# One of two column chunks of the expert rows arrives already turned, as two f16 halves, by a transposing DMA

## The chip, the core and the metric

One of the eight cores of one Trainium2 chip runs the whole program. The metric is the device time of one execution in microseconds (us). The engines are PE (TensorE, matrix products; its weight loads are listed as PEld), DVE (VectorE), ACT (ScalarE), POOL (GpSimd), and SP (SyncE), which here only issues DMAs and waits. An engine's name with a q (SPq, POOLq) is its instruction queue.

## The reference

```
x = x + L0_xattn(ctx, layernorm(x))          # 16 heads
x = x + L0_ffn(layernorm(x))                 # all 8 experts, weighted by their counts
x = x + L1_xattn(layernorm(x), ctx, ctx, mask)
x = x + L1_ffn(layernorm(x), ...)

def L1_ffn(x, W1, b1, W2, b2, Wg, bg):       # 3584 tokens, 256 columns, 8 experts, hidden 512
    gate_logits = xt @ Wg.T + bg
    w, idx = top_k(gate_logits, 2);  w = softmax(w)
    h = relu(einsum('td,ehd->eth', xt, W1) + b1[:, None, :])
    y = einsum('eth,eoh->eto', h, W2) + b2[:, None, :]
    comb = (one_hot(idx, 8) * w[..., None]).sum(axis=1)
    return einsum('eto,te->to', y, comb)
```

The kernel works out only the two experts that a token chose. The change lies in this last part: the rows that are sent to the experts, and how an expert reads them.

## The kernel before, in words

**Three phases.** The attention phase (up to some 450 us), the middle phase (dense mixture, second attention, layer norm and routing; some 450 to 776 us), and the expert stage (some 776 to 985 us). Inside a phase each engine runs its own written-out list of instructions; semaphores order them.

**Middle phase, one step per batch of 112 tokens, 32 batches.** The steps are pipelined: in step u the mixture works on batch u, attention on batches u-4 and u-5, the norm and the gate on u-6 (`ur`), and the sending on u-7 (`uk`). After the last mixture seven more steps drain this pipeline. For a routed batch ACT writes the normalised row `rows[.., 0:256]` in fp32 (L1689), TensorE turns it (L1604), ACT and DVE split the turned row into f16 halves for the gate (`xT_hi` L1698, `xT_lo` L1830). POOL writes the token number (L1518), the combine weights (L1524) and the slots (L1526), updates the running counts (`cum`, L1528), and one step later sends the row twice by indirect DMA (`scatter`, L1475) to the `dispatch` array in DRAM: a row is 272 fp32 words (256 values, 8 weights, the token number, padding). After the last batch a count of tokens on PE (L1640) and a chain of small DVE operations (L1845 to L1902) make the table that tells the expert stage where its rows lie.

**Expert stage.** The sent rows are cut into 63 units of 128 rows. Units 0 to 47 go in pairs of the same expert (24 turns, `paired`); 15 single units make the last 8 turns. For each turn SP loads the rows (L2000 a pair, L2004 a single unit) into one of 4 slots of `rows_e`; a slot is free when the turn four before has written its `y` (`y_rdy`, the wait at L1998, whose instruction is listed as L61). In turns 4 to 18 SP also copies the W1 halves of one single unit inside SBUF (L2009, two copies of 256 KB). PE turns the rows (`turn_rows`, L2048: for a pair two chunks of 128 columns times two units, four fp32 transposes) in the middle of the `up` of the turn before; ACT and DVE split the turned values into f16 halves (`x_hi` L2143, `x_lo` L2187); `up` makes 24 products a pair turn (L2065, hi*hi, hi*lo, lo*hi), ACT applies bias and relu, and `down` (L2100) makes 24 more. DVE adds the bias and scales by the weight (L2209, L2214), and POOL adds each unit's `y` into the output by an indirect DMA (L2035). Such an add may have to wait until the adds of the units before have landed (L2027 to L2033), where the expert changes.

Of the kernel before, what the change touches and what calls it, by code (L numbers as in the profile page):

```python
# [19 lines left out]
E = 8  # L20
# [69 lines left out]
def attention_phase(nc, ctx, dram, keep):  # L90
# [153 lines left out]
    with nc.Block(no_gpsimd_drain=True) as block:  # L244
# [179 lines left out]
        def _(pe):  # L424
# [219 lines left out]

            def maxima_turned(b):            run_steps(pe, step)
# [610 lines left out]
def middle_phase(nc, ctx, dram, keep):  # L1256
# [53 lines left out]
    def reuse(*shape):  # L1310
# [17 lines left out]
    x3 = we[:].rearrange("p c e h -> p (c e h)")[0:S, DC * D * E // 2:DC * D * E // 2 + 2 * D].rearrange("p (n d) -> p n d", d=D)  # L1328
# [5 lines left out]
    w_hi, w_lo = keep["w_hi"], keep["w_lo"]  # L1334
    route_w = sb("route_w", [128, DC, E], F32)
# [18 lines left out]
        cum_rdy token_rdy scattered0 scattered1 scattered2 scattered3 x3_out0 x3_out1 pads_out w_in0 w_in1 w_hi_rdy w_lo_rdy rows_set late_in tally_done table  # L1354
# [41 lines left out]
    with nc.Block(no_gpsimd_drain=True) as block:  # L1396
# [60 lines left out]
        def _(pool):  # L1457
# [27 lines left out]
            def step(t, u, on):  # L1485
# [8 lines left out]
                if r:  # L1494

                    ur = u - LAG_ROUTE
                    v = cnt(t, ur, 1, 1)
                    rstd("ag3", "eps3", "rs3", 1, v)
                    wait(pool, m["rs3"], v)
                    wait(pool, m["x3n_rdy"], cnt(t, ur - 1, 1, 1))  # L1500
# [12 lines left out]
                if r:  # L1513

                    ur = u - LAG_ROUTE
                    wait(pool, scattered[ur % ROW_SLOTS], sent(t, ur - ROW_SLOTS))
                    apart(pool)
                    nc.gpsimd.tensor_scalar(rows[:, ur % ROW_SLOTS, AT_TOKEN:AT_TOKEN + 1], rows[:, ur % ROW_SLOTS, AT_TOKEN:AT_TOKEN + 1],  # L1518
                                            float(ROW_SLOTS * S), None, ALU.add).then_inc(m["token_rdy"], 1)
# [16 lines left out]
        def _(pe):  # L1536
# [24 lines left out]
            def step(t, u, on):  # L1561
# [38 lines left out]
                if r:  # L1600
                    wait(pe, m["x3n_rdy"], cnt(t, ur, 1, 1))
# [47 lines left out]
        def _(act):  # L1649
# [7 lines left out]
            def step(t, u, on):  # L1657
# [25 lines left out]
                if r:  # L1683
# [5 lines left out]
                    nc.scalar.activation(rows[:, ur % ROW_SLOTS, 0:D], x3[:, ur % 2, :], ACT.Identity, bias=ln_shift[:, 1, :],  # L1689
# [5 lines left out]
                if r:  # L1695
                    b0 = (t * TURN + ur) * S
                    wait(act, m["x3nT_done"], cnt(t, ur, 1, 1))
                    nc.scalar.activation(xT_hi[:, :, bass.ds(b0, S)], psum[:, 7, 0:DC * S].rearrange("p (c s) -> p c s", c=DC), ACT.Copy).then_inc(m["x3hi_rdy"], 1)  # L1698

# [3 lines left out]
        def _(dve):  # L1703
# [32 lines left out]
            def step(t, u, on):  # L1736
# [80 lines left out]
                if o:  # L1817
# [3 lines left out]
                    wait(dve, m["x3n_rdy"], cnt(t, uo - 2, 1, 1))  # L1821
# [84 lines left out]
def expert_phase(nc, ctx, dram, keep):  # L1906
# [20 lines left out]
    rows = sb("rows_e", [128, ROW_TURNS, PAIR, ROW], F32)  # L1927
    token_at = sb("token_at", [128, TOKEN_TURNS, PAIR], U32)
    x_hi = sb("x_hi", [128, 2, DC, PAIR * UNIT], F16)
    x_lo = sb("x_lo", [128, 2, DC, PAIR * UNIT], F16)  # L1930
# [13 lines left out]
    names = """pads_sent pads_rdy own_in passed rows_in0 rows_in1 rows_in2 rows_in3 xT_done xhi_rdy xlo_rdy up_done0 up_done1 h_rdy0 h_rdy1  # L1944
# [3 lines left out]
    rows_in = [m[f"rows_in{n}"] for n in range(ROW_TURNS)]  # L1948
# [37 lines left out]
    with nc.Block(no_gpsimd_drain=True) as block:  # L1986

        @block.sync
        def _(sp):
            sp.sem_inc(m["pads_rdy"], 1)  # L1990
            for n in range(TURNS):
# [4 lines left out]
                else:  # L1996
                    sp.wait_ge(m["pads_rdy"], 2)
                wait(sp, m["y_rdy"], finished(n - ROW_TURNS + 1))  # L1998
                if paired(n):
                    sp.dma_start(rows[:, n % ROW_TURNS, :, :],  # L2000
                                 dram["dispatch"][bass.ds(start[0], PAIR * UNIT), :].rearrange("(s p) r -> p s r", p=UNIT)).then_inc(rows_in[n % ROW_TURNS], 16)
                else:
                    for s in units(n):
                        sp.dma_start(rows[:, n % ROW_TURNS, s, :], dram["dispatch"][bass.ds(start[s], UNIT), :]).then_inc(rows_in[n % ROW_TURNS], 16)  # L2004
# [36 lines left out]
        def _(pe):  # L2041
            def turn_rows(n):
# [3 lines left out]
                for kc in range(DC):  # L2046
                    for s in units(n):
                        last = nc.tensor.transpose(psum[:, 0, (kc * PAIR + s) * UNIT:(kc * PAIR + s + 1) * UNIT],  # L2048
                                                   rows[:, n % ROW_TURNS, s, kc * 128:(kc + 1) * 128], ident[:, :])
                last.then_inc(m["xT_done"], 1)  # L2050

            def up_pair(n, e, then):

                wait(pe, m["xlo_rdy"], n + 1)
                for c in range(HC):
# [7 lines left out]
                    for w, x in ((w1_hi, x_hi), (w1_hi, x_lo), (w1_lo, x_hi)):  # L2063
                        for kc in range(DC):
                            last = nc.tensor.matmul(psum[:, 1 + c // 2, c % 2 * PAIR * UNIT:(c % 2 + 1) * PAIR * UNIT],  # L2065
                                                    w[:, bass.ds(e, 1), kc, c * 128:(c + 1) * 128].rearrange("p o h -> p (o h)"),
                                                    x[:, n % 2, kc, :], start=(done == 0), stop=(done == 3 * DC - 1))
# [4 lines left out]
            def up_unit(n, s, then):  # L2072
# [4 lines left out]
                if s == 0:  # L2077
                    wait(pe, m["xlo_rdy"], n + 1)
                for c in range(HC):
# [5 lines left out]
                    for w, x in ((own_hi, x_hi), (own_hi, x_lo), (own_lo, x_hi)):  # L2085
                        for kc in range(DC):
                            last = nc.tensor.matmul(up_bank(s, c), w[k][:, kc, c * 128:(c + 1) * 128], x[:, n % 2, kc, s * UNIT:(s + 1) * UNIT],
# [49 lines left out]
        def _(act):  # L2137
            def high_x(n):
# [4 lines left out]
                nc.scalar.activation(x_hi[:, n % 2, :, 0:width], psum[:, 0, 0:DC * PAIR * UNIT].rearrange("p (c s) -> p c s", c=DC)[:, :, 0:width],  # L2143
                                     ACT.Copy).then_inc(m["xhi_rdy"], 1)
# [38 lines left out]
        def _(dve):  # L2183
            def low_x(n):
                width = len(units(n)) * UNIT
                wait(dve, m["xhi_rdy"], n + 1)
                nc.vector.tensor_tensor(x_lo[:, n % 2, :, 0:width], psum[:, 0, 0:DC * PAIR * UNIT].rearrange("p (c s) -> p c s", c=DC)[:, :, 0:width],  # L2187
                                        x_hi[:, n % 2, :, 0:width], ALU.subtract).then_inc(m["xlo_rdy"], 1)
# [16 lines left out]
            def finish(n, s, e):  # L2205
# [8 lines left out]
                nc.vector.tensor_scalar(y[:, unit % SLOTS, :], y_sum[:, s, :], rows[:, n % ROW_TURNS, s, bass.ds(e + AT_W, 1)], None,  # L2214
                                        ALU.mult).then_inc(m["y_rdy"], 1)

            def tokens(n):
# [3 lines left out]
                                      rows[:, n % ROW_TURNS, 0:len(units(n)), AT_TOKEN:AT_TOKEN + 1]).then_inc(m["token_rdy"], 1)  # L2221
# [147 lines left out]
```

## Time and profile before

| | us |
|---|---|
| median of 3 runs (lowest, highest) | 984.41 (982.87, 990.5) |
| the profiled execution, its own time | 987.03 |
| its span, first to last instruction | 984.9 |
| PE busy / PEld busy | 900.4 / 668.7 |
| DVE / ACT / POOL busy | 730.3 / 543.4 / 551.4 |
| mean granted TensorE clock, of full speed | 0.958 |

The span is what the trace shows; the execution took 2.1 us more than its span. Busy times are shares of the whole program, which has phases with different limits, so they say little by themselves: the phase in question has to be looked at alone.

### The profile page before, as it was taken

The page shows a single profiled execution, that of the slowest core. Times are in us where ns is not written, and L with a number is a line of the kernel's source. Part 1 is how long each engine was busy: PE and PEld are TensorE (multiplying, and loading weights), DVE is VectorE, ACT ScalarE, POOL GpSimd, SP SyncE. Part 2 cuts the span into 40 slices and gives each one's busy share as a digit, 9 for nine tenths or more (in the row PEclk, how much of TensorE's full clock was granted, in tenths as well). Part 3 has the DMA queues.
Part 4 walks back from the last instruction along what each step waited for, and adds up shares of the span by engine and source line. Part 5 has one row for each costly group of instructions (what it writes and reads, how often), then busy time and mean ns, then how long its engine had stood idle before and what let it go on. Part 6 is the DMA issues. An engine that isn't in the chain of part 4 may idle for free. (4 is left out here: it accounts for less than half of the span.)

```text
span 984.9 us, 31478 instructions
## 1 busy us (share of the span) xinstructions
PE 900.4 (91%) x10664; PEld 668.7 (68%) x10664; DVE 730.3 (74%) x2071; ACT 543.4 (55%) x1068; POOL 551.4 (56%) x897
## 2 busy tenths in 40 slices
PE   4799999999999999986999999999976399999993
PEld 2477777777777777754466666666644289889892
DVE  6688888888888888866778888888865356666773
ACT  3377777777777777654044444444443065555551
POOL 6655555565555555401037777777776535556536
PEclk9899999999999999987999999999996599999997
DMA  5644554445444454331565555665552348786535
GB/s 157 178 128 142 144 147 134 135 144 147 125 139 141 142 142 144 94 105 47 141 179 174 183 186 186 189 191 184 175 190 90 120 100 197 176 187 105 96 64 59
DMA packets 107278, 140.56 MB, mean 143 GB/s; under 512 B 23929, under 2 KB 92592, under 8 KB 106928
## 3 DMA queue, kind: packets, MB, share of 16 engines
q1 hardware_dynamic: 94594, 121.38, 41.3%
q0 software_dynamic: 12528, 17.18, 9.7%
q8 instruction: 89, 1.46, 0.6%
q14 instruction: 67, 0.55, 0.2%
HBM read 93.38 MB, written 38.35 MB: 134 GB/s over the span
## 5 line engine op out<-in xcount | busy, mean ns | idle before, releaser
L999 DVE TENSOR_REDUCE smax<-psum 112x2 f32<-112x750 f32 x240 | 216.3, 933 | 24.5 <-PE psum L439 24.4
L840 ACT ACTIVATE probsT<-psum 125x896 f32<-125x896 f32 x173 | 158.7, 917 | 22.0 <-PE psum L454 20.6
L2035 POOL DMA_INDIRECT out_dram<-y,token_at x63 | 101.6, 1612 | 93.9 <-DMA out_dram<-y,token_at 42.2
L1733 DVE SCALAR_TENSOR_TENSOR acc<-psum,neg_bias,acc 128x448 f32<-128x448 f32 x112 | 75.9, 680 | 10.9 <-PE psum L1556 9.3
L1475 POOL DMA_INDIRECT dispatch_dram<-rows,slots_at x64 | 64.0, 1000 | 28.4 <-issue 28.4
L439 PE MATMUL psum<-k_stack,q_stack 63*128 63x375 f16 x480 | 69.3, 326 | 3.9 <-DVE smax L999 2.8
L1556 PE MATMUL psum<-xT_hi,we_hi 128*128 128x448 f16 x256 | 70.2, 356 | 1.1 <-ACT we_hi L1655 1.1
L476 PE MATMUL psum<-probsT,v_aug 125*32 125x112 f32 x2688 | 70.2, 260 | 0.1
L1556 PE MATMUL psum<-xT_lo,we_hi 128*128 128x448 f16 x256 | 69.8, 355 | 0.0
L1556 PE MATMUL psum<-xT_hi,we_lo 128*128 128x448 f16 x256 | 69.7, 354 | 0.0
L476 PEld LDWEIGHTS psum<-probsT,v_aug 125*32 125x32 f32 x2688 | 63.5, 110 | 8.9 <-ACT v_aug L866 8.5
L454 PE MATMUL psum<-q_stack,k_stack 64*128 64x112 f16 x1384 | 63.8, 211 | 2.9 <-DMA q_stack<-neg_max 2.9
L2167 ACT ACTIVATE h<-psum,b 128x256 f32<-128x256 f32 x96 | 40.1, 471 | 38.9 <-PE psum L2065 34.3
L573 PE MATMUL psum<-wv_hi,we 128*125 128x256 f16 x384 | 59.3, 276 | 0.9 <-ACT we L860 0.8
L357 POOL TENSOR_SCALAR ln_var<-ln_mv 112x1 f32<-112x1 f32 x32 | 7.2, 224 | 92.8 <-DVE ln_mv L1011 92.8
L408 POOL TENSOR_TENSOR k_lo<-we,k_hi 128x375 f16<-128x375 f32 x64 | 55.9, 874 | 5.1
L454 PEld LDWEIGHTS psum<-q_stack,k_stack 64*128 64x128 f16 x1384 | 44.3, 95 | 21.1 <-issue 12.6
L1662 ACT ACTIVATE probs<-probs,exp_bias 112x375 f32<-112x375 f32 x32 | 19.4, 607 | 67.8 <-DVE exp_bias L1756 67.8
L553 PE MATMUL psum<-we,wk_hi 128*128 128x375 f16 x256 | 53.8, 334 | 2.9 <-ACT we L860 1.5
L2203 DVE TENSOR_TENSOR h_lo<-h,h_hi 128x512 f16<-128x512 f32 x63 | 41.3, 688 | 17.0 <-ACT h_hi L2153 13.5
L1591 PE MATMUL psum<-ctx_rows,probsT 125*112 125x256 f32 x192 | 50.3, 401 | 2.9 <-issue 2.9
L365 POOL TENSOR_TENSOR we<-we 128x750 f16<-128x750 f32 x32 | 51.5, 1609 | 1.1 <-ACT we L847 1.1
(298 smaller groups left out, 2448.3 us busy)
## 6 DMA issues: line engine op xcount, KB each, us to landing
k_stack<-k_hi_dram SPq DMA_DIRECT2D x64, 188.0 KB, 2.8
we<-in_ctxT_dram SPq DMA_DIRECT2D x32, 375.0 KB, 3.5
ctxT<-in_ctxT_dram SPq DMA_DIRECT2D x32, 375.0 KB
ctx_rows<-in_ctx_dram SPq DMA_DIRECT2D x32, 375.0 KB
w_raw<-in_w_dram SPq DMA_DIRECT2D x32, 256.0 KB, 3.9
rows_e<-dispatch_dram SPq DMA_DIRECT2D x24, 272.0 KB
k_hi_dram<-k_hi SPq DMA_DIRECT2D x32, 188.0 KB, 2.8
k_lo_dram<-k_lo SPq DMA_DIRECT2D x32, 188.0 KB, 2.7
```

What stands on the lines that cost most here:

```text
L408: nc.gpsimd.tensor_tensor(k_lo[:, u % 2, mc, 0:KV], k_full[:, mc, :], k_hi[:, u % 2, mc, 0:KV], ALU.subtract).then_inc(m["klo_ready"], 1)
L439: last = nc.tensor.matmul(psum[:, pair_bank(s) + a, 0:KV], queries(rows, b4, s, 128), keys_at(rows, b4, s, 0, KV), start=True, stop=True)
L454: last = nc.tensor.matmul(psum[:, a, r * S:(r + 1) * S], keys_at(rows, b4, 4 * hg + r, c * KC, 128), queries(rows, b4, 4 * hg + r, S), sta ...
L476: last = nc.tensor.matmul(bank_d[32 * j:32 * j + 32, g * S:(g + 1) * S], v_aug[:, b4d, cc, h, :], probsT[:, b2d, cc, h // 8, h % 2, h // 2 ...
L553: last = nc.tensor.matmul(bank_a[:, 0:KV], w[:, kc, mc * 128:(mc + 1) * 128], x[:, b2a, kc, :], start=(n == 0), stop=(n == 3 * DC - 1))
L573: last = nc.tensor.matmul(bank[0:KC, n * D:(n + 1) * D], x[:, b2a, kc, cc * KC:(cc + 1) * KC], w[:, kc, :], start=(done == 0), stop=(done ...
L840: nc.scalar.activation(probsT[:, p, c, hg, :, :, :].rearrange("p k h q -> p k (h q)"), psum[0:KC, 0:2, 0:4 * S], ACT.Exp, scale=float(HD) ...
L999: nc.vector.reduce_max(smax[:, (u - LAG_B) % 2, 2 * (s % 4) + s // 4::PAIRS], psum[0:S, pair_bank(s):pair_bank(s) + 2, 0:KV], AX.X).then_i ...
L1475: nc.gpsimd.indirect_dma_start(dram["dispatch"], bass.IndirectOffsetOnAxis(slots_at[:, b % ROW_SLOTS, n:n + 1], 0), rows[:, b % ROW_SLOTS, ...
L1556: last = nc.tensor.matmul(psum[:, mix_bank(t, u, k), 0:GT], w[:, kc, e, hc * 128:(hc + 1) * 128], x[:, kc, bass.ds(g0, GT)], start=(n == 0 ...
L1733: nc.vector.scalar_tensor_tensor(out, psum[:, mix_bank(t, u, k), 0:GT], neg_bias[:, hc, e:e + 1], out, ALU.max, ALU.add).then_inc(m["acc_r ...
L2035: nc.gpsimd.indirect_dma_start(dram["out"], bass.IndirectOffsetOnAxis(token_at[:, unit // PAIR % TOKEN_TURNS, unit % PAIR:unit % PAIR + 1] ...
```

## The change

In the middle phase the first 128 columns of a sent row are no longer fp32: their 512 bytes hold 128 f16 high halves and 128 f16 low halves. ACT writes the second 128 columns as before, the first 128 into a small buffer `x3n`, and the high half as a copy of it; POOL makes the low half by a subtraction. In the expert stage SP loads columns 128 and on as before (144 words of a row in place of 272), and issues two transposing DMAs for a pair turn (four for a turn of two single units), which bring the two halves of the first chunk into `x_hi[0]` and `x_lo[0]` with the columns on the partitions. TensorE turns only the second chunk, and ACT and DVE split only that. `x_hi[0]` and `x_lo[0]` have 4 slots in place of 2. PE waits for the transposed halves (`x_in`) at the start of `up`. From turn 4 on SP issues a turn's transposing DMAs ahead of its wait for `y`, in turns 0 to 3 behind the rows. The first hunk takes out a second, never called definition of a function.

```diff
@@ middle phase, POOL
+                if k:
+                    uk = u - LAG_SEND
+                    wait(pool, m["x3hi_rdy"], cnt(t, uk, 2, 2))
+                    nc.gpsimd.tensor_tensor(rows_lo[:, uk % ROW_SLOTS, :], x3n[:, uk % 2, :], rows_hi[:, uk % ROW_SLOTS, :],
+                                            ALU.subtract).then_inc(m["row_rdy"], 1)
@@ middle phase, PE
                     for kc in range(DC):
-                        last = nc.tensor.transpose(psum[:, 7, kc * S:(kc + 1) * S], rows[:, ur % ROW_SLOTS, kc * 128:(kc + 1) * 128], ident[0:S, 0:S])
+                        half_row = x3n[:, ur % 2, :] if kc == 0 else rows[:, ur % ROW_SLOTS, 128:D]
+                        last = nc.tensor.transpose(psum[:, 7, kc * S:(kc + 1) * S], half_row, ident[0:S, 0:S])
@@ middle phase, ACT
-                    nc.scalar.activation(rows[:, ur % ROW_SLOTS, 0:D], x3[:, ur % 2, :], ACT.Identity, bias=ln_shift[:, 1, :],
+                    nc.scalar.activation(rows[:, ur % ROW_SLOTS, 128:D], x3[:, ur % 2, 128:D], ACT.Identity, bias=ln_shift[:, 1, :],
+                                         scale=ln_rstd[:, 1, :]).then_inc(m["x3n_rdy"], 1)
+                    wait(act, m["row_rdy"], cnt(t, ur - 2, 2, 2))
+                    nc.scalar.activation(x3n[:, ur % 2, :], x3[:, ur % 2, 0:128], ACT.Identity, bias=ln_shift[:, 1, :],
                                          scale=ln_rstd[:, 1, :]).then_inc(m["x3n_rdy"], 1)
...
+                    nc.scalar.activation(rows_hi[:, ur % ROW_SLOTS, :], x3n[:, ur % 2, :], ACT.Copy).then_inc(m["x3hi_rdy"], 1)
@@ expert stage, SP
+                def transposed():
+                    wait(sp, up_done[0], 2 * (n - ROW_TURNS + 1))
+                    wait(sp, up_done[1], 2 * (n - ROW_TURNS + 1 - DOUBLES))
+                    for s, at in enumerate(start):
+                        width = PAIR * UNIT if paired(n) else UNIT
+                        for half, x in enumerate((x_hi, x_lo)):
+                            sp.dma_start(x_of(x, n, 0, s * UNIT, width), halves[bass.ds(at, width), half * 128:(half + 1) * 128],
+                                         transpose=True).then_inc(x_in[n % ROW_TURNS], 16)
+
+                if n >= ROW_TURNS:
+                    transposed()
                 wait(sp, m["y_rdy"], finished(n - ROW_TURNS + 1))
                 if paired(n):
                     sp.dma_start(rows[:, n % ROW_TURNS, :, :],
-                                 dram["dispatch"][bass.ds(start[0], PAIR * UNIT), :].rearrange("(s p) r -> p s r", p=UNIT)).then_inc(rows_in[n % ROW_TURNS], 16)
+                                 dram["dispatch"][bass.ds(start[0], PAIR * UNIT), 128:ROW].rearrange("(s p) r -> p s r", p=UNIT)).then_inc(rows_in[n % ROW_TURNS], 16)
...
+                if n < ROW_TURNS:
+                    transposed()
@@ expert stage, PE, turn_rows and up_pair
-                for kc in range(DC):
-                    for s in units(n):
-                        last = nc.tensor.transpose(psum[:, 0, (kc * PAIR + s) * UNIT:(kc * PAIR + s + 1) * UNIT],
-                                                   rows[:, n % ROW_TURNS, s, kc * 128:(kc + 1) * 128], ident[:, :])
+                for s in units(n):
+                    last = nc.tensor.transpose(psum[:, 0, s * UNIT:(s + 1) * UNIT], rows[:, n % ROW_TURNS, s, 0:128], ident[:, :])
...
+                wait(pe, x_in[n % ROW_TURNS], 2 * rows_arrived(n))
                 wait(pe, m["xlo_rdy"], n + 1)
```

SP's list for one of the turns 4 to 18 before (TENSOR_LOAD is a look-up in the table):

```order
L1964 TENSOR_LOAD table
L1964 ISA x2
L2000 ISA
L2000 DMA rows_e<-dispatch_dram 128x2x272
L2009 ISA
L2009 DMA xT_lo<-w_hi 128x1024
L2009 REGISTER_ALU
L2009 DMA spare_w<-w_lo 128x1024
```

and with the change:

```order
L1977 TENSOR_LOAD table
L1977 ISA x2
L2021 ISA
L2021 DMA_TRANSPOSE x_hi<-dispatch_dram 128x256
L2021 DMA_TRANSPOSE x_lo<-dispatch_dram 128x256
L2028 ISA
L2028 DMA rows_e<-dispatch_dram 128x2x144
L2039 ISA
L2039 DMA xT_lo<-w_hi 128x1024
L2039 REGISTER_ALU
L2039 DMA spare_w<-w_lo 128x1024
```

Two more DMAs stand in SP's list for a turn, between the look-ups and the load of the rows.

PE's list in the middle of the `up` of a pair turn before:

```order
L2065 MATMUL psum<-x_hi,w_lo 128x256
L2048 MATMUL psum<-ident,rows_e 128x128 x4
L2065 ISA
L2065 MATMUL psum<-x_hi,w_hi 128x256
L2065 MATMUL psum<-x_lo,w_hi 128x256 x2
```

and with the change:

```order
L2094 MATMUL psum<-x_hi,w_lo 128x256
L2077 MATMUL psum<-ident,rows_e 128x128 x2
L2094 ISA
L2094 MATMUL psum<-x_hi,w_hi 128x256
L2094 MATMUL psum<-x_lo,w_hi 128x256 x2
```

Two of the four transposes are gone; nothing else on PE has moved.

POOL's list in a step of the middle phase before, from the sending of the batch before on:

```order
L1475 DMA dispatch_dram<-rows,slots_at 30208x272 x2
L1511 TENSOR_TENSOR w_lo<-w_raw,w_hi 128x512
L1518 TENSOR_SCALAR rows<-rows 112x1
L1524 TENSOR_SCALAR rows<-unscaled,first_w 112x8
L1526 CAST slots_at<-slots 112x2
L1528 TENSOR_TENSOR cum<-cum,chosen 112x8
```

and with the change:

```order
L1475 DMA dispatch_dram<-rows,slots_at 30208x272 x2
L1508 TENSOR_TENSOR rows<-we,rows 112x128
L1516 TENSOR_TENSOR w_lo<-w_raw,w_hi 128x512
L1523 TENSOR_SCALAR rows<-rows 112x1
L1529 TENSOR_SCALAR rows<-unscaled,first_w 112x8
L1531 CAST slots_at<-slots 112x2
L1533 TENSOR_TENSOR cum<-cum,chosen 112x8
```

One subtraction has come in ahead of the weight split and the counts.

## Rows read from the trace of the kernel before

**Rows 1.** Stretches of the program: busy us per engine, granted clock, DMA share, GB/s.

```profile
core 0: us, PE busy (x) PEld busy (x) DVE busy (x) ACT busy (x) POOL busy (x), PEclk, DMA share, GB/s
500.00:720.00 220.00, 219.40 (x1317) 144.76 (x1315) 180.30 (x765) 95.12 (x233) 154.30 (x328) 1.00 0.59 182
720.00:777.80 57.80, 30.86 (x146) 20.97 (x146) 31.72 (x192) 18.54 (x46) 38.75 (x82) 0.70 0.36 114
800.00:888.00 88.00, 87.60 (x800) 78.53 (x799) 55.37 (x122) 51.52 (x109) 49.04 (x30) 1.00 0.81 187
888.00:928.00 40.00, 39.76 (x388) 35.97 (x386) 25.86 (x62) 22.99 (x49) 23.22 (x15) 1.00 0.58 98
```

**Rows 2.** Chain that ended last, its first and last pieces: start, us, what.

```profile
928.60 0.33 DVE y_sum L2209
...
932.11 3.87 DMA out_dram<-y,token_at
...
976.83 3.56 DMA out_dram<-y,token_at
```

**Rows 3.** Timeline of PE, pair turns: start, us, line, operation, count.

```profile
785.95 1.06 PE L2048 MATMUL psum<-ident,rows_e 128*128 128x128 f32 x4
786.80 0.53 PE L2065 MATMUL psum<-x_hi,w_hi 128*128 128x256 f16 x2
...
906.13 0.60 PE L2048 MATMUL psum<-ident,rows_e 128*128 128x128 f32 x4
906.57 0.38 PE L2065 MATMUL psum<-x_hi,w_hi 128*128 128x256 f16 x2
...
911.81 0.60 PE L2048 MATMUL psum<-ident,rows_e 128*128 128x128 f32 x4
```

**Rows 4.** Timeline of SP's queue, turns with own copies.

```profile
804.56 0.39 SPq L2000 DMA_DIRECT2D rows_e<-dispatch_dram  x1
...
810.26 0.38 SPq L2000 DMA_DIRECT2D rows_e<-dispatch_dram  x1
811.35 0.50 SPq L2009 DMA_DIRECT2D xT_hi<-w_hi  x1
811.97 0.53 SPq L2009 DMA_DIRECT2D we<-w_lo  x1
```

**Rows 5.** Waits of SP's queue, 800 to 885 us: total us, times, longest.

```profile
SPq L61 <- DVE y L2214: 16.8, 11, 2.5
```

**Rows 6.** Issues of the pads to the output by SP: ns min/median/max.

```profile
L1417 SPq DMA_DIRECT2D out_dram<-in_pads_dram x5: 589/597/597, 478.1 to 480.7; - x5
```

**Rows 7.** DMA queue of SP (q1), 800 to 888 us: packets, MB, share of 16 engines.

```profile
q1 hardware_dynamic: 8663, 12.31, 43.8%
```

**Rows 8.** The same, 888 to 928 us.

```profile
q1 hardware_dynamic: 1952, 1.95, 18.3%
```

**Rows 9.** The expert stage's start: SP's first load, PE's first transposes and products.

```profile
777.80 21.58 SPq L2000 DMA_DIRECT2D rows_e<-dispatch_dram  x5
...
780.77 1.12 PE L2048 MATMUL psum<-ident,rows_e 128*128 128x128 f32 x4 [5.53 <-DMA rows_e<-dispatch_dram]
783.39 0.60 PE L2065 MATMUL psum<-x_hi,w_hi 128*128 128x256 f16 x2 [1.50 <-issue]
```

**Rows 10.** Timeline of POOL, middle phase: a steady step, the draining, the last batches.

```profile
721.45 0.22 POOL L1481 TENSOR_SCALAR ln_var<-ln_mv 112x1 f32<-112x1 f32 x1 [0.66 <-DVE ln_mv L1745]
...
729.50 0.22 POOL L1481 TENSOR_SCALAR ln_var<-ln_mv 112x1 f32<-112x1 f32 x1 [0.19 <-DVE ln_mv L1745]
...
769.15 0.19 POOL L1528 TENSOR_TENSOR cum<-cum,chosen 112x8 f16<-112x8 f16 x1
```

**Rows 11.** Two subtractions of POOL: ns min/median/max.

```profile
L408 POOL TENSOR_TENSOR k_lo<-we,k_hi x64: 847/886/902, 17.0 to 412.1; 128x375 f16<-128x375 f32 x64
L1511 POOL TENSOR_TENSOR w_lo<-w_raw,w_hi x32: 1149/1170/1177, 486.9 to 751.0; 128x512 f16<-128x512 f32 x32
```

**Rows 12.** Groups by shape, ACT: busy us, mean ns, idle before.

```profile
L1689 ACT ACTIVATE rows<-we,ln_shift,ln_rstd 112x256 f32<-112x256 f32 x32 | 19.2, 600 | 18.8 <-POOL ln_shift L1502 18.8
```

More of the change, by code:

```diff
@@ L1334, in middle_phase @@
     w_hi, w_lo = keep["w_hi"], keep["w_lo"]
+    rows_hi, rows_lo = (rows[:].bitcast(F16)[:, :, n * 128:(n + 1) * 128] for n in range(2))
     route_w = sb("route_w", [128, DC, E], F32)
@@ L1499, in step @@
                     wait(pool, m["rs3"], v)
-                    wait(pool, m["x3n_rdy"], cnt(t, ur - 1, 1, 1))
+                    wait(pool, m["x3n_rdy"], cnt(t, ur - 1, 2, 2))
                     apart(pool)
@@ L1698, in step @@
                     nc.scalar.activation(xT_hi[:, :, bass.ds(b0, S)], psum[:, 7, 0:DC * S].rearrange("p (c s) -> p c s", c=DC), ACT.Copy).then_inc(m["x3hi_rdy"], 1)
+                    wait(act, m["x3n_rdy"], cnt(t, ur, 2, 2))
+                    apart(act)
+                    nc.scalar.activation(rows_hi[:, ur % ROW_SLOTS, :], x3n[:, ur % 2, :], ACT.Copy).then_inc(m["x3hi_rdy"], 1)
             steps(act, step)
@@ L1925, in expert_phase @@
     b1, b2, pad_at, pad_rows, table = (keep[k] for k in ("b1", "b2", "pad_at", "pad_rows", "table"))
-    rows = sb("rows_e", [128, ROW_TURNS, PAIR, ROW], F32)
+    rows = sb("rows_e", [128, ROW_TURNS, PAIR, ROW - 128], F32)
     token_at = sb("token_at", [128, TOKEN_TURNS, PAIR], U32)
-    x_hi = sb("x_hi", [128, 2, DC, PAIR * UNIT], F16)
-    x_lo = sb("x_lo", [128, 2, DC, PAIR * UNIT], F16)
+    x_hi = [sb(f"x_hi{kc}", [128, slots, PAIR * UNIT], F16) for kc, slots in enumerate((ROW_TURNS, 2))]
+    x_lo = [sb(f"x_lo{kc}", [128, slots, PAIR * UNIT], F16) for kc, slots in enumerate((ROW_TURNS, 2))]
+    halves = dram["dispatch"].bitcast(F16)
     h = sb("h", [128, PAIR, HC, UNIT], F32)
@@ L1947, in expert_phase @@
     m = {n: sem("x_" + n) for n in names}
-    rows_in = [m[f"rows_in{n}"] for n in range(ROW_TURNS)]
+    rows_in, x_in = ([m[f"{k}{n}"] for n in range(ROW_TURNS)] for k in ("rows_in", "x_in"))
     added = [m[f"added{n}"] for n in range(SLOTS)]
@@ L2066, in up_pair @@
                                                     w[:, bass.ds(e, 1), kc, c * 128:(c + 1) * 128].rearrange("p o h -> p (o h)"),
-                                                    x[:, n % 2, kc, :], start=(done == 0), stop=(done == 3 * DC - 1))
+                                                    x_of(x, n, kc, 0, PAIR * UNIT), start=(done == 0), stop=(done == 3 * DC - 1))
                             done += 1
@@ L2077, in up_unit @@
                 if s == 0:
+                    wait(pe, x_in[n % ROW_TURNS], 2 * rows_arrived(n))
                     wait(pe, m["xlo_rdy"], n + 1)
@@ L2142, in high_x @@
                 width = len(units(n)) * UNIT
-                nc.scalar.activation(x_hi[:, n % 2, :, 0:width], psum[:, 0, 0:DC * PAIR * UNIT].rearrange("p (c s) -> p c s", c=DC)[:, :, 0:width],
-                                     ACT.Copy).then_inc(m["xhi_rdy"], 1)
+                nc.scalar.activation(x_of(x_hi, n, 1, 0, width), psum[:, 0, 0:width], ACT.Copy).then_inc(m["xhi_rdy"], 1)
             def high_h(n, s):
@@ L2220, in tokens @@
                 nc.vector.tensor_copy(token_at[:, n % TOKEN_TURNS, 0:len(units(n))].rearrange("p (n o) -> p n o", o=1),
-                                      rows[:, n % ROW_TURNS, 0:len(units(n)), AT_TOKEN:AT_TOKEN + 1]).then_inc(m["token_rdy"], 1)
+                                      rows[:, n % ROW_TURNS, 0:len(units(n)), AT_TOKEN - 128:AT_TOKEN - 127]).then_inc(m["token_rdy"], 1)
             def experts(n):
```

29 lines of the change are left out of this document (15 added, 14 removed).

## The prediction

> **What bounds the kernel now.** I began with the chain of waits. It names only the end [rows 2]: from 928.60 us on the program follows the indirect adds into the output, nine landings in a row (first and last are shown), each add waiting for the one before. What starts this chain is the `y` of the last pair turn, so what comes earlier counts only as far as it moves that point. The stretches [rows 1] show what does: from 800 to 928 us PE is busy for 87.60 of 88 us and 39.76 of 40 us at the full granted clock, while DVE, ACT and POOL have a third or more to spare. The timeline [rows 3] has one pair turn from transpose to transpose, 906.13 to 911.81, so 5.68 us. DMA is the second thing to see there: its share is 0.81 while the weights of the single units are copied, 0.58 afterwards. The middle phase is PE's too (219.40 of 220 us), but from 720 to 777.8 us it drains: PE is busy for 30.86 of 57.80 us, and the chain passes from engine to engine.
>
> **TensorE.** The four transposes of a pair turn hold PE from 906.13 to 906.57 [rows 3], 0.44 us; two are left, so 0.22 us a turn, and a turn of 5.46 us if PE goes on setting it. Ahead of the point at 928.60 us lie the transposes of turns 1 to 24: 24 x 0.22 = 5.3 us is the most that PE can give. The later single turns save as much, but there the chain of adds is waited for, not PE, so that counts nothing. The narrower split on ACT and DVE lies beside PE and counts nothing.
>
> **The stage's start.** From the first transpose to the first product it takes 783.39 - 780.77 = 2.62 us [rows 9]; TensorE is still slow there, and the four transposes of the next turn take 786.80 - 785.95 = 0.85 us [rows 3], so half of them saves 0.43, and the narrower splits a little more: up to 0.9 us. But PE now needs the transposed halves as well, issued behind the rows. The first load was issued at 777.80 and used at 780.77, 2.97 us later [rows 9]. With the second half issued 1.2 to 2 us after it, it arrives at about 782 to 783, about when the split is done. I take -0.5; the ends are -0.9 and +3.
>
> **SP, where the change adds.** In a turn with copies of weights SP's turn is 810.26 - 804.56 = 5.70 us [rows 4]. Its free time is what it waits for `y`: 16.8 us in 11 waits, 1.53 us each [rows 5]; if the other four of the 15 turns truly have none, 1.12 a turn. So its own work is 4.17 us, or 4.58. Two transposing DMAs come on top, ahead of the wait, and the load of the rows is queued behind them: SP's turn becomes that work plus 2T, T being the time that SP takes to issue one. The trace has no such issue. The nearest rows are plain issues: 0.38 us for 256 rows, 0.50 and 0.53 for the copies [rows 4], 0.59 for DRAM to DRAM, the dearest undisturbed one [rows 6]. Below 0.38 nothing speaks for it; above, no row bounds it, so the upper end is a rival. A transposing DMA has more to lay out than a plain one, so I take 0.6. That makes 4.17 + 1.2 = 5.37 us, under PE's 5.46, or 4.58 + 1.2 = 5.78, over it. I take 5.6, between the two: 15 turns x (5.60 - 5.70) = -1.5 us. The other nine turns save 9 x 0.22 = 2.0 us.
>
> **The DMA engines.** From 888 to 928 us SP's queue takes 18.3% of 40 us for four pair loads and six single ones, seven pairs' worth [rows 8]: 1.05 us of all engines for 272 KB, 265 GB/s. In the earlier stretch, where the copies of weights raise the queue's share to 43.8% [rows 7], a turn leaves 0.19 x 5.70 = 1.08 us free, and the shorter rows give back between nothing (if a row costs the same) and 0.49 us (by bytes). The transposed 128 KB thus have room for 1.08 to 1.57 us, which is 121 to 84 GB/s; at the rate of the row loads they take 0.49. I cost this at nothing, with that cover. The page DMA: Bandwidth & Descriptors of the Trainium skill, section Latency and other measured facts, gives 261 GB/s for a transposing DMA with a non-contiguous middle dimension; by it the halves would take 0.50 us, an estimate, and no run here shows it yet.
>
> **The middle phase.** POOL's subtraction is 128 columns wide. Its like took 886 ns for 375 columns and 1170 ns for 512 [rows 11], 2.07 ns a column, so 0.37 us. In a steady step POOL waits 0.66 us for DVE [rows 10] and PE sets the pace: nothing, with that cover. While the pipeline drains the wait is 0.19 us, so 0.18 comes through in each of four steps, and in the last two, where POOL's own list leads to the counts that end at 769.15, all of it: 4 x 0.18 + 2 x 0.37 = 1.5 us; the ends are 0.7 and 3. ACT's one normalisation of 256 columns (600 ns) [rows 12] becomes two of 128. If each cost half the sum is unchanged, if each cost as much as the whole, 0.6 us more in some seven draining steps: 0 to 4.2 us. The columns are the same in sum, so I take 0.5, near the first. The copy to f16 stands behind `xT_hi`, where ACT next waits for DVE: nothing.
>
> **The sum.** -1.5 - 2.0 - 0.5 + 1.5 + 0.5 = -2.0 us. The profiled execution took 987.03 us (span 984.9), which is 2.6 above the median of 984.41 and inside its range; against it the change would make 985.0, against the median 982.4. I forecast **982 us**. With T at 0.38 (PE's 5.46 us holds in 15 turns, so -3.6 in place of -1.5) and the cheap ends of the middle phase it is 979; with SP's turn at 5.78 and the dear ends 994.
>
> **Rival 1, the slower side: SP's queue sets the turn.** Place: the two transposing DMAs ahead of the load of the rows, turns 4 to 18. Price: 15 x (4.17 + 2T - 5.70). T = 1.5 gives 15 x 1.47 = 22 us, and with the other terms (-2.0 - 0.5 + 2.0) 1006 us; T = 2 gives +37 and 1021. It decides from T = 0.65 on, and 9.8 us (1%) are reached at T = 1.11. For it: SP has only these 1.1 to 1.5 us a turn to give, and the load of the rows stands behind both transposing DMAs. Against it: no plain issue is over 0.6 us undisturbed. Chance 0.38, of which 0.26 beyond T = 1.11.
>
> **Rival 2: the turning is slow in the DMA engines.** A pair turn has four halves of 128 x 128. If they are turned one after another, PE gets one turn's worth every four of these times, and from 1.37 us each (5.46 / 4) that sets the turn. By rows, if the two DMAs of a turn follow one another, each like the first load's 2.97 us, a turn is 5.94: 24 x (5.94 - 5.70) = 5.8, and with -0.5 and +2.0 it makes 992; if each of the four took that long, 11.9 us a turn and over 1100. If they are spread but move at a quarter of the row loads' rate, 1.98 us a turn, it overruns the room by 0.4 to 0.9 us: +6 to +13 in 15 turns, 990 to 997. For it: each half is 256 rows of only 256 bytes. Against it: DMA is idle for 0.19 to 0.42 of the time. Chance 0.14, of which 0.12 slower by over 1%. The page VectorE: DVE Perf Modes of the Trainium skill, section The three transpose paths, speaks against the change: 390 ns for such a block on TensorE, 1309 ns by the DMA crossbar; four of these would be an estimated 5.24 us, just within PE's turn. The trace's 0.11 us a transpose in a stream [rows 3] is cheaper still than the page's figure for TensorE.
>
> **Rival 3: faster by over 1%.** The nine landings sum to 36.7 us; if lighter loads brought all to the shortest, 3.56 us [rows 2], that gave another 4.6; with SP hidden (15 x 0.24 = 3.6, and 2.0 and 0.5) and a free middle phase it reaches 10.7 us and 974. All of it must come together. Chance 0.06. That TensorE would still turn both chunks is excluded by its list of instructions.
>
> **How the numbers follow.** The forecast has 0.42, its own range 977 to 990. A measurement of this kernel can tell about 1%, 9.8 us, from no change. Slower: 0.26 + 0.12 = 0.38. Faster: 0.06. The same: 0.42 + 0.12 + 0.02 = 0.56. The range reaches from 975 (leaving out most of rival 3) to 1015 (T up to about 1.8).
>
> **What would show it.** The step on PE is right if the transposes of a pair turn hold it for 0.22 us and turns are 5.46 to 5.7 us apart. T is read off SP's queue; its waits for `y` from 800 to 885 us should fall from 16.8 us to near nothing. Rival 1 shows as no such wait left, turns over 5.8 us, and PE waiting for `rows_e`; rival 2 as PE waiting for `x_hi` and a DMA share near 1; the middle phase as a longer stretch from 720 us to the table. I am wrong if T is over 1.1 us, or if a transposing DMA holds up the others in its queue.

## The result, and the profile after

The changed kernel takes 1017.18 us (median of 4 runs, 1013.88 to 1017.99), the kernel before in the same comparison 985.67 us (4 runs, 982.87 to 990.5): a ratio of 1.030, 95% interval 1.027 to 1.033. It is slower by 31.5 us, and outside the predicted range of 975 to 1015. The profiled execution after took 1013.88 us with a span of 1012.1; before it was 987.03 and 984.9, so 27 us is what the two traces can explain.

The stretches, in the columns of [rows 1]:

```profile
core 0: us, PE busy (x) PEld busy (x) DVE busy (x) ACT busy (x) POOL busy (x), PEclk, DMA share, GB/s
500.00:720.00 220.00, 218.39 (x1311) 144.03 (x1310) 180.29 (x764) 106.90 (x284) 163.93 (x353) 1.00 0.59 181
720.00:778.86 58.86, 30.07 (x146) 20.12 (x146) 31.37 (x190) 20.77 (x58) 41.07 (x88) 0.72 0.35 111
800.00:888.00 88.00, 73.08 (x633) 61.86 (x630) 42.70 (x103) 39.94 (x91) 38.95 (x25) 0.98 0.75 154
888.00:928.00 40.00, 36.63 (x316) 31.90 (x317) 20.33 (x50) 18.79 (x44) 19.41 (x13) 0.96 0.71 123
```

Up to 720 us PE is nearly as full as before (218.39 us for 219.40); ACT and POOL are busy 11.8 and 9.6 us longer there, with the added work. The draining stretch is 1.06 us longer (58.86 for 57.80). Then PE, which had been full from 800 to 888 us, is idle for 14.9 of 88 us, and no other engine took over: DVE, ACT and POOL all do less, the DMA share fell from 0.81 to 0.75, and the granted clock is nearly the same (0.98 for 1.00). An idle stretch with no busy engine in it points to a queue. PE's waits name one (total us, times, longest): first those of before for 800 to 928 us, then those after the change for 800 to 928 and for 928 to 1012:

```profile
PE psum L2048 <- DMA rows_e<-dispatch_dram: 0.2, 1, 0.2
```

```profile
PE psum L2077 <- DMA rows_e<-dispatch_dram: 17.7, 13, 2.6
```

```profile
PE psum L2077 <- DMA rows_e<-dispatch_dram: 11.4, 6, 2.6
```

PE waits for the rows, which are loaded by a plain DMA, and not for the transposed halves. The rows are late because their load stands behind two transposing DMAs in SP's queue. SP's timeline of one turn with copies of weights, in answer to [rows 4]:

```profile
861.18 1.12 SPq L2021 DMA_TRANSPOSE x_hi<-dispatch_dram  x1
862.44 1.21 SPq L2021 DMA_TRANSPOSE x_lo<-dispatch_dram  x1
863.85 0.42 SPq L2028 DMA_DIRECT2D rows_e<-dispatch_dram  x1
865.00 0.51 SPq L2039 DMA_DIRECT2D xT_lo<-w_hi  x1
865.63 0.53 SPq L2039 DMA_DIRECT2D spare_w<-w_lo  x1
868.01 1.16 SPq L2021 DMA_TRANSPOSE x_hi<-dispatch_dram  x1
```

From 861.18 to 863.85 the two transposing DMAs hold SP for 2.67 us, T = 1.33 us each with the register work between them; the whole turn is 868.01 - 861.18 = 6.83 us. The rest, 4.16 us, is SP's other work, as it was read from before. All issues of the kind together (ns min/median/max), and under them what SP waits for `y` in all of 800 to 1012 us, where [rows 5] had 16.8 us in 85 us:

```profile
L2021 SPq DMA_TRANSPOSE x_hi<-dispatch_dram x39: 767/1125/2579, 779.4 to 985.9; - x39
L2021 SPq DMA_TRANSPOSE x_lo<-dispatch_dram x39: 695/1147/2290, 780.8 to 987.0; - x39
```

```profile
SPq L2028 <- DVE y L2242: 1.3, 1, 1.3
```

SP has next to no free time left. In the turns of single units it is worse, since each has four transposing DMAs, and these take as long for 128 rows as the others for 256:

```profile
938.28 1.12 SPq L2021 DMA_TRANSPOSE x_hi<-dispatch_dram  x1
939.53 1.14 SPq L2021 DMA_TRANSPOSE x_lo<-dispatch_dram  x1
940.80 1.15 SPq L2021 DMA_TRANSPOSE x_hi<-dispatch_dram  x1
942.08 1.15 SPq L2021 DMA_TRANSPOSE x_lo<-dispatch_dram  x1
943.43 0.95 SPq L2032 DMA_DIRECT2D rows_e<-dispatch_dram  x2
945.72 1.11 SPq L2021 DMA_TRANSPOSE x_hi<-dispatch_dram  x1
```

That is 7.44 us a turn where PE had taken some 6.0 before (from turn 25 to 31). Where SP is not the bound, PE's gain is there as predicted. In turns 20 to 23, which have no copies, the transposes of two turns in a row, in answer to [rows 3], stand 5.46 us apart, and the first product follows 0.22 us after them:

```profile
909.88 0.38 PE L2077 MATMUL psum<-ident,rows_e 128*128 128x128 f32 x2
910.10 0.38 PE L2094 MATMUL psum<-x_hi,w_hi 128*128 128x256 f16 x2
...
915.34 0.38 PE L2077 MATMUL psum<-ident,rows_e 128*128 128x128 f32 x2
```

The table puts the loss in its place: the start of the transposes of some turns, read from PE's timeline of each kernel; e1 to e9 are the experiments told below. Turns 4 to 18 have the copies, 24 to 31 the single units.

| kernel | turn 0 | turn 4 | turn 19 | turn 24 | turn 31 | span | us a turn, 4 to 19 | us a turn, 24 to 31 |
|---|---|---|---|---|---|---|---|---|
| before | 780.77 | 803.09 | 889.10 | 917.49 | 960.36 | 984.9 | 5.73 | 6.12 |
| after | 781.29 | 803.76 | 909.88 | 939.61 | 995.15 | 1012.1 | 7.07 | 7.93 |
| e1 | 781.11 | 803.82 | 889.81 | 920.68 | 974.54 | 991.5 | 5.73 | 7.69 |
| e2 | 781.76 | 804.06 | 905.04 | 934.00 | 981.81 | 1000.0 | 6.73 | 6.83 |
| e3 | 781.87 | 806.57 | 894.27 | 922.66 | 965.64 | 987.8 | 5.85 | 6.14 |
| e4 | 780.31 | 803.41 | 891.62 | 918.91 | 960.53 | 983.9 | 5.88 | 5.95 |
| e5 | 782.73 | 806.44 | 890.37 | 917.66 | 958.60 | 987.2 | 5.60 | 5.85 |
| e7 | 781.81 | 804.37 | 910.39 | 938.09 | 979.83 | 1003.2 | 7.07 | 5.96 |
| e9 | 782.84 | 805.83 | 891.06 | 918.36 | 959.45 | 982.6 | 5.68 | 5.87 |

After against before: +0.7 us up to turn 4, +20.1 from 4 to 19, +1.3 to turn 24 (the gain of 0.22 us in each of four turns, and then the first single turn, late by 2.2), +12.7 from 24 to 31. At the end 7.6 us come back: the adds, which before came last by a long chain [rows 2], are now caught up by the products, and the chain of waits begins only here:

```profile
1002.07 0.50 DVE y L2242
...
1007.73 1.55 POOL out_dram L2065
```

### The profile page after: what moved, and what is told of

The parts are those of the page before. It is cut to its first block and busy times, and to the rows that moved or that the text cites. A ratio compares the mean times of both kernels' runs of the same rounds, so it can differ in the third digit from the quotient of the medians.

```text
span 1012.1 us, 31638 instructions
## 1 busy us (share of the span) xinstructions
PE 904.3 (89%) x10601; PEld 663.8 (66%) x10601; DVE 721.5 (71%) x2071; ACT 551.3 (54%) x1132; POOL 560.3 (55%) x929
## 5 line engine op out<-in xcount | busy, mean ns | idle before, releaser
L2065 POOL DMA_INDIRECT out_dram<-y,token_at x63 | 98.9, 1571 | 122.6 <-DVE y L2242 73.0
L1475 POOL DMA_INDIRECT dispatch_dram<-rows,slots_at x64 | 64.0, 1000 | 28.6 <-issue 28.6
L2216 DVE TENSOR_TENSOR x_lo<-psum,x_hi 128x256 f16<-128x256 f32 (+1 forms) x32 | 13.4, 420 | 57.1 <-ACT x_hi L2173 42.6
```

Of the source, the lines that this page charges most:

```text
L2065: nc.gpsimd.indirect_dma_start(dram["out"], bass.IndirectOffsetOnAxis(token_at[:, unit // PAIR % TOKEN_TURNS, unit % PAIR:unit % PAIR + 1] ...
```

## The experiments

Theory A: SP issues a transposing DMA for some 1.13 us (1.3 with its register work) whatever its size, and this serial time sets the turn, in turns 4 to 18 and in the single turns. Theory B: the turning is slow in the DMA engines, and SP is only held up by it. Theory C: the middle phase carries a good part. Each ratio is to the kernel before on the same chip in the same comparison.

**e2, time on SP and nothing else.** To the kernel before, look-ups of a table entry are added at the head of SP's turns:

```diff
             for n in range(TURNS):
+                if n >= ROW_TURNS:
+                    for _ in range(4 * len(loads(n))):
+                        look_up(sp, 1, PAIR * n, 0, DISPATCH_ROWS)
```

> The kernel before with nothing but time added on SP: four more look-ups of the table (some 0.7 us each) at the head of each pair turn from turn 4 on, eight in each turn of single units; no DMA is added or moved, and nothing else differs. Theory A: SP's list is 4.2 + 2.7 = 6.9 us, so turns 4 to 18 are 6.7 to 7.2 us apart and the time is that of the changed kernel, 1008 to 1022 us, with PE waiting for rows_e. Theory B: SP's time alone does little: under 995 us.

Measured: 1001.99 us, ratio 1.015 (1.011 to 1.018). A turn from 4 to 19 took 6.73 us, and PE waited for the rows as in the changed kernel. SP's turn, and PE's waits from 800 to 928 us:

```profile
848.80 0.39 SPq L2003 DMA_DIRECT2D rows_e<-dispatch_dram  x1
849.90 0.50 SPq L2012 DMA_DIRECT2D xT_lo<-w_hi  x1
850.52 0.54 SPq L2012 DMA_DIRECT2D spare_w<-w_lo  x1
855.20 0.39 SPq L2003 DMA_DIRECT2D rows_e<-dispatch_dram  x1
```

```profile
PE psum L2051 <- DMA rows_e<-dispatch_dram: 11.0, 11, 2.0
```

The turn shown is 855.20 - 848.80 = 6.40 us; the loads of turns 4 to 18 are 6.81 us apart on average, 2.6 us above SP's work of 4.16 or 4.17. So 2.6 us of pure SP time in a pair turn, without a byte more on the DMA engines, gives 15.9 of the 20.8 us by which turn 19 came late after the change. The time expected was too high: it came out 6 us under the range. In the single turns the look-ups cost less than the four transposing DMAs (6.83 us a turn for 7.93), and the changed kernel's longer issues (up to 2.58 us) have no counterpart here.

**e1, the copies on another queue.** The changed kernel, with the look-up and the two copies of a single unit's weights issued by ACT:

```diff
-                if ROW_TURNS <= n < ROW_TURNS + SINGLES:
-                    k = n - ROW_TURNS
-                    e = look_up(sp, 0, PAIR * DOUBLES + k, 0, E - 1)
-                    for own, w in ((own_hi, w1_hi), (own_lo, w1_lo)):
-                        sp.dma_start(own[k], w[:, bass.ds(e, 1), :, :].rearrange("p o c h -> p (o c) h")).then_inc(m["own_in"], 16)
...
+                    if c == 1 and ROW_TURNS <= n < ROW_TURNS + SINGLES:
+                        k = n - ROW_TURNS
+                        own_e = look_up(act, 0, PAIR * DOUBLES + k, 0, E - 1)
+                        act.dma_start(own_hi[k], w1_hi[:, bass.ds(own_e, 1), :, :].rearrange("p o c h -> p (o c) h")).then_inc(m["own_in"], 16)
...
+                if ROW_TURNS <= n < ROW_TURNS + SINGLES:
+                    k = n - ROW_TURNS
+                    act.dma_start(own_lo[k], w1_lo[:, bass.ds(own_e, 1), :, :].rearrange("p o c h -> p (o c) h")).then_inc(m["own_in"], 16)
```

On ACT the first copy stands behind the two activations that open a turn, the second at the turn's end.

> The changed kernel with the copies of the single units' weights (one look-up and two 256 KB copies in each of turns 4 to 18) issued by ACT instead of SP; all DMA traffic stays. Theory A (SP's serial time, about 1.3 us for each transposing DMA, sets the turn): SP's own list falls from 6.83 us by the 1.85 us of look-up and copies to about 5.0, so turns 4 to 18 go back to 5.4 to 5.7 us (PE's 5.46, or ACT's list, which has 1.8 us a turn to spare and gets that much more), and turn 19's transpose comes at 885 to 890 us, not 909.9. The single turns, with four transposing DMAs each on SP, still lose: 985 to 1000 us in all. Theory B (the turning itself is slow in the DMA engines and SP's issue is only held up by it): turns 4 to 18 stay at 6.8 to 7.1 us, 1010 to 1020 us.

Measured: 994.13 us, ratio 1.006 (1.004 to 1.009). With all transposing DMAs and all bytes still there, turn 19 is back at 889.81 us, 20.1 us earlier than after the change. SP waits for `y` again (800 to 885 us), and the DMA engines, at a share of 0.75 after the change, turn out to have room for 0.93:

```profile
SPq L2028 <- DVE y L2244: 6.5, 7, 1.5
```

```profile
800.00:888.00 88.00, 84.66 (x768) 74.86 (x766) 49.87 (x121) 48.02 (x109) 47.21 (x30) 1.00 0.93 177
```

Theory B said 6.8 to 7.1 us a turn and falls. The mean turn of 5.73 us is above PE's 5.46 because a few were longer, two of them 6.9 and 7.5 us. In the first of these PE waited 1.31 us for rows that SP had issued 4.7 us earlier, after a wait for `y`:

```profile
850.26 0.39 SPq L2028 DMA_DIRECT2D rows_e<-dispatch_dram  x1
```

```profile
854.98 0.44 PE L2072 MATMUL psum<-ident,rows_e 128*128 128x128 f32 x2 [1.31 <-DMA rows_e<-dispatch_dram]
```

So at a DMA share of 0.93 a load can land late although SP was free; what held it was not tried. The single turns, whose queue was not relieved, still took 7.69 us.

**e4, half the instructions for the same bytes.** The high and the low halves of a row lie side by side, and one transposing DMA turns 256 columns into two blocks:

```diff
-                        for half, x in enumerate((x_hi, x_lo)):
-                            sp.dma_start(x_of(x, n, 0, s * UNIT, width), halves[bass.ds(at, width), half * 128:(half + 1) * 128],
-                                         transpose=True).then_inc(x_in[n % ROW_TURNS], 16)
+                        sp.dma_start(x_first[:, n % ROW_TURNS, :, s * UNIT:s * UNIT + width], halves[bass.ds(at, width), 0:256],
+                                     transpose=True).then_inc(x_in[n % ROW_TURNS], 16)
```

> The changed kernel with the high and the low halves of the first chunk turned by one transposing DMA (256 columns into two blocks of 128 partitions) where there were two: the same bytes, half the instructions. Theory A (a fixed price per instruction on SP, about 1.15 us whatever its size): SP's list falls from 6.83 by 1.3 to about 5.5 us, pair turns to 5.46 to 5.7, the single turns' SP list from 7.9 to 5.3: 979 to 990 us in all. Theory B (the price belongs to the data that are turned): one instruction takes 2.2 to 2.7 us, or the halves land later, turns stay at 6.6 to 7.1 us, 1005 to 1020 us.

Measured: 987.35 us, ratio 1.001 (0.999 to 1.003). The whole loss is gone. The instruction with twice the columns costs SP 6 to 8% more, and SP's turn is 6.12 us here:

```profile
L2020 SPq DMA_TRANSPOSE x_first<-dispatch_dram x39: 652/1215/1733, 778.5 to 950.2; - x39
```

```profile
850.77 1.23 SPq L2020 DMA_TRANSPOSE x_first<-dispatch_dram  x1
852.21 0.40 SPq L2027 DMA_DIRECT2D rows_e<-dispatch_dram  x1
853.36 0.52 SPq L2038 DMA_DIRECT2D xT_lo<-w_hi  x1
854.00 0.53 SPq L2038 DMA_DIRECT2D spare_w<-w_lo  x1
856.89 1.22 SPq L2020 DMA_TRANSPOSE x_first<-dispatch_dram  x1
```

The price is one per instruction, nearly whatever its columns; why it is so high is open. SP, which never waits for `y` there from 800 to 885 us, still sets turns 4 to 18 in the main (5.88 us on average; its loads of rows are 5.94 us apart), though PE's waits from 800 to 928 us are 2.0 us for rows and 2.7 for ACT's `h`; in the single turns PE sets it again.

**e7, the same in the single turns alone.**

```diff
+                        if not paired(n):
+                            sp.dma_start(x_first[:, n % ROW_TURNS, :, s * UNIT:s * UNIT + width], halves[bass.ds(at, width), 0:256],
+                                         transpose=True).then_inc(x_in[n % ROW_TURNS], 16)
+                            continue
                         for half, x in enumerate((x_hi, x_lo)):
```

> The changed kernel with one transposing DMA for both halves in the turns of single units (24 to 31) only; the pair turns keep two. Theory A: pair turns as in the changed kernel (turn 24 at 938 to 942 us), then SP's list in single turns falls from 7.9 to 5.3 us and these turns from 7.9 to about 5.6 to 6.0 us: the time is 11 to 15 us below the changed kernel's 1017, so 1002 to 1006 us. If, as the prediction said, the later single turns count nothing since the chain of adds is waited for: 1014 to 1019 us.

Measured: 1005.88 us, ratio 1.021 (1.017 to 1.024). Turns 4 to 19 are those of the changed kernel (7.07 us), the single turns fall from 7.93 to 5.96, and 11.3 us of the 31.5 are gone (9.3 by the two ratios). The single turns' share is shown by this, and the prediction's word that they count nothing falls.

**e9, plain DMAs in the place of the transposing ones.** Same rows, same columns, same place in SBUF:

```diff
-                            sp.dma_start(x_of(x, n, 0, s * UNIT, width), halves[bass.ds(at, width), half * 128:(half + 1) * 128],
-                                         transpose=True).then_inc(x_in[n % ROW_TURNS], 16)
+                            sp.dma_start(x_of(x, n, 0, s * UNIT, width).rearrange("p (u c) -> p u c", c=128),
+                                         halves[bass.ds(at, width), half * 128:(half + 1) * 128].rearrange("(u p) c -> p u c", p=UNIT)).then_inc(x_in[n % ROW_TURNS], 16)
```

> The changed kernel with each transposing DMA replaced by a plain one that moves the same 128 columns of halves of the same rows to the same place, not turned (so the products are not those of the reference). Theory A (the transposing form has the price on SP): each issue takes 0.4 to 0.55 us, SP's list is 4.2 + 1.1 to 1.3 = 5.3 to 5.5 us, turns 4 to 18 are 5.5 to 5.9 us, single turns 5.6 to 6.2: 983 to 993 us. Theory D (any further DMA on SP costs the turn as much, by its bytes or its count): turns stay at 6.6 to 7.1 us and the time over 1008 us.

Measured: 983.5 us, ratio 0.996 (0.994 to 0.999). The issues (ns min/median/max):

```profile
L2021 SPq DMA_DIRECT2D x_hi<-dispatch_dram x39: 4/346/1181, 781.1 to 949.4; - x39
...
L2021 SPq DMA_DIRECT2D x_lo<-dispatch_dram x39: 297/372/1546, 781.6 to 950.0; - x39
```

So the transposing form, not the number of DMAs or their bytes, is what SP pays for: 1.13 us for 0.35 to 0.37. What the DMA engines pay can be read from SP's queue (q1) from 800 to 888 us, here and in e4, where the turns are nearly as long (packets, MB, share of 16 engines; first e9, then e4):

```profile
q1 hardware_dynamic: 16106, 11.94, 44.6%
```

```profile
q1 hardware_dynamic: 16023, 11.92, 47.5%
```

Three points of the share for the same bytes. The page Advanced Engine Details and Errata of the Trainium skill, section X-Bar Transpose (TRN2), says that transposing DMAs are as fast as regular ones; for the DMA engines these rows agree within those three points, and for the queue that issues them the two medians above speak against it.

**e3, the middle phase alone.** The changed kernel with its expert stage taken back to that of before.

```diff
-    rows = sb("rows_e", [128, ROW_TURNS, PAIR, ROW - 128], F32)
+    rows = sb("rows_e", [128, ROW_TURNS, PAIR, ROW], F32)
...
-                if n >= ROW_TURNS:
-                    transposed()
...
```

> The middle phase of the changed kernel (the first 128 columns of a row written as f16 halves) with the expert stage of the kernel before, which reads those columns as fp32 numbers, so the values of the expert stage are not those of the reference; its work and its traffic are. Theories A and B alike: the tally is written about 1 us later (770.4 against 769.4 us), pair turns stay at 5.68 us, 984 to 989 us in all, a ratio of 1.000 to 1.004. Theory C (the middle phase carries a good part of the loss, or spoils the expert stage): over 992 us.

Measured: 990.52 us, ratio 1.004 (1.003 to 1.006), between what A and B gave it and what C did. In its trace SP's first load is 1.4 us later, and 2.4 us more are lost in turns 1 to 3: TensorE, which waits for the first rows, is granted less of its clock from 786 to 798 us:

```profile
786.00:792.00 6.00, 4.50 (x25) 3.37 (x24) 0.69 (x1) 2.55 (x6) 1.80 (x2) 0.70 0.42 121
792.00:798.00 6.00, 5.71 (x37) 4.46 (x36) 1.58 (x4) 2.44 (x6) 0.00 (x0) 0.72 0.01 3
```

Before, the same two rows have 0.91 and 1.00, and after the change 0.94 and 1.00. So the 1.06 us of the changed kernel's own trace are the middle phase, and this second loss is not in it; that it belongs to the change is not shown.

**e5, e1 and e4 together.** This is the version to which they point.

```diff
+                        sp.dma_start(x_first[:, n % ROW_TURNS, :, s * UNIT:s * UNIT + width], halves[bass.ds(at, width), 0:256],
+                                     transpose=True).then_inc(x_in[n % ROW_TURNS], 16)
...
+                        act.dma_start(own_hi[k], w1_hi[:, bass.ds(own_e, 1), :, :].rearrange("p o c h -> p (o c) h")).then_inc(m["own_in"], 16)
```

> Both earlier edits together: one transposing DMA for both halves, and the copies of the single units' weights issued by ACT. With one DMA alone, SP's list still stood at 5.6 to 6.1 us in turns 4 to 18 and SP never waited for y there; with the copies on ACT it falls to about 4. Theory A: every pair turn at PE's 5.46 us (ACT's list, 5.5 us, may hold some), turn 24's transposes at 912 to 915 us against 917.5 before, single turns 5.5 to 5.9 us: 979 to 985 us in all, a ratio of 0.993 to 0.999. Theory B (the DMA engines, which carry the same bytes, were what held the turns at 5.9): turns 4 to 18 stay at 5.7 to 6.1 us and the ratio at 1.000 or above. Also possible: the gain arrives at turn 24 and is lost in the chain of adds at the end.

Measured: 984.27 us, ratio 0.997 (0.995 to 0.999): it beats the changed kernel by 3% and the kernel before by 0.3% (0.1 to 0.5). The pair turns are PE's again for the most part (5.60 us on average, 5.46 in the last five), and SP's free time is larger than ever (waits for `y`, 800 to 885 us):

```profile
912.21 0.38 PE L2071 MATMUL psum<-ident,rows_e 128*128 128x128 f32 x2
917.66 0.38 PE L2071 MATMUL psum<-ident,rows_e 128*128 128x128 f32 x2
```

```profile
SPq L2027 <- DVE y L2243: 29.1, 13, 5.8
```

From turn 4 to turn 31 it takes 152.16 us where before took 157.27, 5.1 us less. In the profiled execution, the longest of its twelve (989.02 us), this is spent: it reaches turn 4 3.4 us later, with the same low clock at the start as e3 (0.66 and 0.72), and the stretch from turn 31 to the end is 28.6 us for 24.5, since the adds into the output, one landing after the other, end no sooner.

## Why the prediction was wrong

**The bound and PE's gain: right.** A pair turn of PE is 5.46 us where nothing else holds it, with 0.22 us for the transposes. One reading is a turn off: the `y` at 928.60 us, with which the chain of adds begins, is that of the first single turn; the last pair turn's were written from 923.28 and 924.17 us. That moves the 5.3 us by 0.2 and no more.

**SP: the step that failed.** The term was T, the time of one issue: "so I take 0.6", next to the "nearest rows", plain issues of 0.38 to 0.59 us. T was 1.33 us, over the 1.1 that the prediction named as the sign of being wrong. The rest of the term held: SP's other work was 4.16 us for the 4.17 worked out from [rows 4, 5], the list came to 6.83, and rival 1's own formula with T = 1.33 gives 15 x (4.17 + 2.67 - 5.70) = 17 us; measured were 20.1, since SP's turns were not all alike: the loads of turns 4 to 18 are 7.09 us apart on average, with one transposing issue of 2.10 us and one load of rows of 1.32 us among them. The rows of plain DMAs bound T only from below, as the text said of them; the forecast was then put next to them all the same. e9 shows the difference between the two forms, e4 that it is paid per instruction.

**The single turns: wrong.** "The later single turns save as much, but there the chain of adds is waited for, not PE, so that counts nothing" may hold for a gain, which no run tries by itself. For a loss it does not: four transposing DMAs a turn made SP's list 7.4 us and more against 6.0, and the chain had room for only a part of that. After the change this cost 12.7 us up to turn 31, of which the end gave back 7.6; e7 gives 9.3 to 11.3 us of the whole time for it. Rival 1 priced 15 turns and left these eight out: at T = 1.33 its sum is 984.4 + 17.1 - 0.5 = 1001 us, and the single turns and the 3.0 us by which the pair turns exceeded the formula bring it to 1013 to 1015; the profiled execution took 1013.88, and the 2 to 4 us up to the median are not accounted for. The range's upper end, 1015, was meant to hold for T up to about 1.8. T stayed below that, and the time lay beyond the end all the same, because the single turns had been left out.

**The DMA engines: right for this result, with a limit.** "I cost this at nothing": PE's waits from 800 us on name no transposed half, and e4 carries the same bytes at the time of before. That their share fell says little, since the turns were longer; at turns of 5.73 us it is 0.93 (e1), and there a load of rows landed late. The 1309 ns that the page VectorE: DVE Perf Modes of the Trainium skill, section The three transpose paths, gives for a block turned by DMA stood under rival 2, as time of the crossbar, four times a turn. The trace has 1.13 us an issue, twice a pair turn, in SP's queue. By that figure four blocks one after another would take an estimated 5.24 us. The trace does not bear this out: the four blocks of turn 0 were issued from 779.42 us on and used at 783.66, 4.24 us later.

**The start: not as taken, but small.** -0.5 was forecast. From SP's first load to the first product it took 783.66 - 778.86 = 4.80 us after, 5.59 before [rows 9], 0.8 better; then turn 1 was late (its load of rows, behind turn 0's two transposing DMAs and look-ups that took longer than before, was issued at 785.73 us, before at 779.81), and turn 4 stood 22.47 us behind turn 0 for 22.32 before.

**The middle phase: near in the sum, not in its terms.** 2.0 us was forecast; SP's first load came 1.06 later, and e3's whole time, 1.003 to 1.006, leaves room for more. The two halves of the normalisation cost 493 and 478 ns, some 0.8 of the whole's price (600 ns [rows 12]) each, so ACT's term was mis-sized: over the prediction's seven steps it would be 7 x 0.37 = 2.6 us for the 0.5 taken, most of which did not come through; POOL's subtraction took 439 ns for 370 forecast:

```profile
L1695 ACT ACTIVATE rows<-we,ln_shift,ln_rstd 112x128 f32<-112x128 f32 x32 | 15.8, 493 | 20.6 <-POOL ln_shift L1502 20.6
L1698 ACT ACTIVATE we<-we,ln_shift,ln_rstd 112x128 f32<-112x128 f32 x32 | 15.3, 478 | 0.0
```

**The rivals.** What came was rival 1, given 0.38, with the signs named for it: next to no wait for `y` left, turns over 5.8 us, PE waiting for `rows_e`. Rival 2's signs, PE waiting for `x_hi` and a DMA share near 1, did not come, and e1 and e4 exclude it as the cause of the long turns.

## What to carry to other kernels

Where a queue has an operation that no row of the profile shows, its slack is what to compare: SP had 1.1 to 1.5 us a turn to give and two unknown issues to take, so the forecast hung on a number that the trace could not hold. Count instructions per turn on the issuing engine in every kind of turn, those with four of them too, before bytes on the DMA engines. When an issue has a fixed price, put more into one instruction, or move other issues to an engine with free time, and only then see what the freed engine is worth: here 5 us of PE's time, of which 2.7 reached the end.

## What the runs showed of the hardware

- A transposing DMA held SP for a median of 1.13 us, for 128 rows as for 256, and 1.22 us with twice the columns (e4); plain DMAs of the same halves held it for 0.35 to 0.37 us (e9). Some took over 2 us, one of them 3.67 us (e1).
- ACT issued the copies of 256 KB in 0.49 to 0.50 us each, with few exceptions up to 0.58 (e1), and its queue did so while an activation ran: one copy was issued from 823.79 to 824.29 us, beside the activation from 823.63 to 824.26.
- One transposing DMA can turn 256 columns into two blocks of 128 partitions at about the issue price of one block (1.22 us for 1.13, e4).
- TensorE's granted clock came back to 1.00 (2.4 GHz) by 792 us in some kernels and was still at a mean of 0.72, a mix of that and 1.2 GHz, from 792 to 798 us in others (e3, e5; 0.73 in e9). Turn 4 then stood 24.70, 23.71 and 22.99 us behind turn 0, for 22.32 before. PE had been waiting for the first rows in all of them; what decides it was not tried.
